# The feed-forward part of an attention block in another order: three chunks of gates at the head, other PSUM banks, and GpSimd on the even gates

## The reference

```python
x = x + layernorm(attention(layernorm(x), ...))
z = layernorm(x)
h = silu((z @ w1.T) * w1_s) * ((z @ w2.T) * w2_s)    # 128 -> 512, the gates
h = gelu((h @ h1.T) * h1_s)                          # 512 -> 512, layer 1
h = gelu((h @ h2.T) * h2_s)                          # 512 -> 512, layer 2
x = x + layernorm((h @ w3.T) * w3_s)                 # 512 -> 128, layer 3
```

## Time and profile before

| | us |
|---|---|
| median of 3 runs (lowest to highest) | 326.47 (325.59 to 327.27) |
| the profiled execution's own time | 327.04 |
| its span, first to last instruction | 325.2 |
| TensorE busy, share of the span | 283.9 (87%) |
| VectorE busy | 217.7 (67%) |
| ScalarE busy | 212.3 (65%) |
| GpSimd busy | 45.2 (14%) |

### The profile page before, as it was taken

The page is one execution under the profiler, slowest core; times in us unless marked ns, Lnnn a source line. Parts: engine busy times, 40 slices in busy tenths (PEclk is TensorE's granted clock), DMA queues, the critical chain, the costliest instruction groups (busy, mean ns, idle before and its releaser), DMA issues.

```text
span 325.2 us, 5036 instructions
## 1 busy us (share of the span) xinstructions
PE 283.9 (87%) x1844; PEld 186.9 (57%) x1844; DVE 217.7 (67%) x451; ACT 212.3 (65%) x313; POOL 45.2 (14%) x52
## 2 busy tenths in 40 slices
PE   8859699989999999999999966789997979699980
PEld 7644363646565555555555533346885758488870
DVE  3855355888789788897888956936558343554485
ACT  2431246678786787857878599547796576767750
POOL 3200400000001001010010137203202110300111
PEclk9985558999999999999999997559999798989997
DMA  6889800533031254522212000000000000010012
GB/s 160 260 248 245 283 2 24 183 109 100 27 89 54 67 194 171 174 87 67 78 31 62 1 3 0 1 0 2 1 2 0 0 0 0 2 32 0 1 35 69
DMA packets 22748, 23.29 MB, mean 72 GB/s; under 512 B 3745, under 2 KB 19905, under 8 KB 22465
## 3 DMA queue, kind: packets, MB, share of 16 engines
q1 hardware_dynamic: 21872, 22.38, 23.5%
q10 hardware_dynamic: 848, 0.54, 0.6%
HBM read 15.93 MB, written 6.68 MB: 70 GB/s over the span
## 4 chain that ended last, share of the span: by engine, by line
PE 52%; DVE 16%; ACT 11%; DMA 8%; issue 6%; SPq 4%; POOL 1%; ACTq 0%; POOLq 0%
PE place L1335 9%; PE place L1336 9%; PE place L1154 8%; PE pv L1204 7%; DVE mx L643 6%; ACT ring L916 5%; PE place L1144 4%; PE place L1180 3%; SPq L429 3%; DMA raw<-ext 2%; PE pv L1335 2%; DVE stats L569 2%; PE pv L1336 2%; DMA k_first<-z_parts 2%; DMA k_parts<-z_parts 2%
## 5 line engine op out<-in xcount | busy, mean ns | idle before, releaser
L643 DVE TENSOR_REDUCE mx<-place 128x4 f32<-128x1024 f32 x64 | 78.3, 1223 | 26.9 <-PE place L1154 25.7
L916 ACT ACTIVATE ring<-place 128x1024 f32<-128x1024 f32 x64 | 65.6, 1026 | 7.8 <-PE place L1191 5.7
L1154 PE MATMUL place<-room,identr 128*128 128x512 f32 x128 | 52.2, 492 | 3.6 <-ACT room L882 3.1
L923 ACT COPY place<-raw 128x1024 f32<-128x1024 f32 x40 | 40.8, 1021 | 16.0 <-DVE mx L643 16.0
L503 POOL TENSOR_TENSOR rstd<-mv,mhalf 128x2 f32<-128x2 f32 (+1 forms) x26 | 21.5, 827 | 205.4 <-DVE mv L577 205.4
L1335 PE MATMUL place<-room,w_hi 128*128 128x512 f32 (+1 forms) x108 | 42.6, 397 | 3.6 <-ACT ring L1026 2.9
L1336 PE MATMUL place<-room,w_hi 128*128 128x512 f32 (+1 forms) x108 | 41.9, 391 | 0.0
L1204 PE MATMUL pv<-ring,vx 128*9 128x256 f32 x512 | 37.0, 411 | 2.0 <-ACT ring L916 1.9
L1144 PE MATMUL place<-room 33*128 33x256 f32 x256 | 31.3, 325 | 8.4 <-ACT ring L916 4.0
L1180 PE MATMUL place<-room 33*128 33x256 f32 x256 | 34.2, 348 | 4.8 <-ACT place L923 3.3
L767 DVE TENSOR_TENSOR room<-ring,room 128x512 fp32r<-128x512 f32 x32 | 21.9, 691 | 22.7 <-ACT room L1028 22.7
(11 more groups left out here) (129 smaller groups left out, 395.7 us busy)
## 6 DMA issues: line engine op xcount, KB each, us to landing
raw<-ext SPq DMA_DIRECT2D x8, 384.0 KB, 7.3
room<-q_parts SPq DMA_DIRECT2D x48, 64.0 KB
room<-k_parts SPq DMA_DIRECT2D x48, 64.0 KB
w_lo<-h SPq DMA_DIRECT2D x2, 1024.0 KB, 5.0
q_parts<-w_hi SPq DMA_DIRECT2D x4, 256.0 KB, 3.1
k_parts<-w_hi SPq DMA_DIRECT2D x2, 512.0 KB, 3.4
xs<-x SPq DMA_DIRECT2D x3, 256.0 KB, 6.3
w_lo<-w SPq DMA_DIRECT2D x3, 256.0 KB, 2.8
```

Of the source, the lines that this page charges most:

```text
L643: nc.vector.tensor_reduce(mx[:, s // RPAIRS, :, :, s % RPAIRS].rearrange("p i k -> p k i"), max_tile(b * PAIRS + s)[:, :, :].rearrange("p ...
L916: nc.scalar.activation(probs[:, s % PRING, :, :, :].rearrange("p k j n -> p (k j n)"), score_tile(b * PAIRS + s)[:, :, :].rearrange("p k n ...
L923: nc.scalar.copy(score_tile(i)[:, :, :].rearrange("p k (j n) -> p k j n", j=2), pair_windows(raw[:, :, :], i % PAIRS)).then_inc(bias_set, 1)
L1154: last = mm(max_tile(b * PAIRS + s)[:, half, :], identr[:, :], windows(table_hi[:, 2 * s + half, :], 0, P, 2, S), start=False, stop=True, ...
```

## The change

The work is the same: as many matmuls, products, gelus and lo parts. What changes:

- TensorE takes the gates of chunks 0, 1 and 2 at the head, with layer 1 of chunk 0 among them one tile at a time. Layer 2 of chunk 1 and layer 1 of chunk 2 no longer have gates inside, but for layer 1 of chunk 2, which has gates 3.2 and 3.3 after its first tile. `norm_T` comes after the first tile of layer 2 of chunk 1.
- The tiles of the layers use other banks, in turn, and so wait for other readers; the slots and halves follow.
- For even gates GpSimd makes hi as well as lo (a copy with a cast, then the subtraction). ScalarE casts only the odd ones.
- VectorE's and ScalarE's lists follow TensorE's order. ScalarE switches tables between silu and gelu twice less, and two switches are asked for early by an activation of one column (`table_ahead`).

The core of the diff (the tuples, GpSimd's function, VectorE's list, ScalarE's list, what gates and layers wait for, TensorE's list):

```diff
-G_SLOT, A1_SLOT, A2_SLOT = (0, 1, 3, 0), (3, 2, 2, 1), (0, 1, 3, 2)
-G_HALF, A1_HALF, A2_HALF = (0, 1, 1, 1), (0, 1, 0, 1), (0, 0, 0, 1)
+G_SLOT, A1_SLOT, A2_SLOT = (0, 1, 2, 1), (3, 0, 0, 3), (1, 3, 2, 1)
+G_HALF, A1_HALF, A2_HALF = (0, 1, 0, 1), (1, 0, 0, 1), (1, 0, 0, 1)
...
-        A1_BANK = ((4, 5, 6, 0), (1, 2, 3, 4), (4, 5, 6, 4), (5, 6, 0, 1))
-        A2_BANK = ((5, 6, 4, 5), (6, 4, 5, 6), (2, 3, 4, 5), (6, 0, 1, 2))
-        Y3_BANK, BACK_BANK = (3, 4), (5, 6)
+        A1_BANK = ((4, 5, 6, 0), (1, 2, 3, 4), (6, 4, 5, 0), (1, 2, 3, 6))
+        A2_BANK = ((5, 6, 0, 1), (2, 3, 4, 5), (4, 5, 0, 1), (2, 3, 6, 4))
+        Y3_BANK, BACK_BANK = (5, 0), (1, 2)
...
-            def gate_low(c):
+            def gate_parts(c):
                 for k in range(0, NK, 2):
-                    pool.wait_ge(g_hi_act, c * NK + k + 1)
+                    pool.wait_ge(gate_set, c * NK + k + 1)
                     hi, lo = parts_of(G_SLOT[c], k)
+                    nc.gpsimd.tensor_copy(hi, act_f[:, G_HALF[c], k, :]).then_inc(g_hi_pool, 1)
+                    pool.wait_ge(g_hi_pool, c * (NK // 2) + k // 2 + 1)
                     nc.gpsimd.tensor_tensor(lo, act_f[:, G_HALF[c], k, :], hi.bitcast(F32),
                                             ALU.subtract).then_inc(g_lo_pool, 1)
...
-            gate_low(1)
+            gate_parts(0)
+            gate_parts(1)
+            gate_parts(2)
             inv_std((B - 1) * 2 + NU + 1, TPB)
             inv_std((B - 1) * 2 + NU + 2, TPB)
-            gate_low(2)
-            gate_low(3)
+            gate_parts(3)
...
+            def gate_product(c, k):
+                dve.wait_ge(silu_done, c * NK + (k + 1))
+                if c == 2:
+                    wait_gate_low(dve, 0, k)
+                elif c == 3:
+                    dve.wait_ge(a2_lo_set, k + 1)
+                nc.vector.scalar_tensor_tensor(
+                    out=act_f[:, G_HALF[c], k, :], in0=bank[GBANK[k % 2][1]], scalar=hs[:, 1, k:k + 1],
+                    in1=gate[:, k % 2, :], op0=ALU.mult, op1=ALU.mult).then_inc(gate_set, 1)
+            def gate_low(c, k):
+                dve.wait_ge(g_hi_act, c * (NK // 2) + k // 2 + 1)
+                hi, lo = parts_of(G_SLOT[c], k)
+                nc.vector.tensor_tensor(lo, act_f[:, G_HALF[c], k, :], hi.bitcast(F32),
+                                        ALU.subtract).then_inc(g_lo_dve, 1)
+            gate_product(0, 0)
+            gate_product(0, 1)
+            gate_product(0, 2)
+            gate_low(0, 1)
+            gate_product(0, 3)
+            gate_product(1, 0)
+            gate_low(0, 3)
+            gate_product(1, 1)
+            gate_product(1, 2)
+            gate_low(1, 1)
             weigh(B - 1, 0)
-            gates(1)
+            gate_product(1, 3)
+            gate_product(2, 0)
+            gate_low(1, 3)
+            gate_product(2, 1)
             weigh(B - 1, 1)
+            gate_product(2, 2)
+            gate_low(2, 1)
+            gate_product(2, 3)
+            gate_low(2, 3)
             layer_low(0, 0)
-            layer_low(1, 0)
             attn_moments(B - 1)
-            layer_low(0, 1, (0, 1))
+            layer_low(1, 0, (0, 1))
             residual(B - 1)
-            layer_low(0, 1, (2, 3))
+            layer_low(1, 0, (2, 3))
             second_norm(B - 1)
+            layer_low(0, 1)
+            layer_low(1, 1, (0, 1))
             z_low(B - 1)
-            gates(2)
-            layer_low(1, 1)
-            gates(3)
+            layer_low(1, 1, (2, 3))
+            gate_product(3, 0)
+            gate_product(3, 1)
+            gate_product(3, 2)
+            gate_low(3, 1)
+            gate_product(3, 3)
+            gate_low(3, 3)
...
-            gates(0)
-            gates(1)
-            layer(0, 0)
+            def table_ahead(function):
+                nc.scalar.activation(table_loaded[:, :], mhalf[:, 0:1], function)
+            for n in range(3 * NK):
+                gate_silu(n // NK, n % NK)
+                if n % 2 == 0 and n > 0:
+                    gate_high((n - 1) // NK, (n - 1) % NK)
+            gate_high(2, NK - 1)
+            layer(0, 0, (0, 1))
             keep_onT(B - 1)
+            layer(0, 0, (2, 3))
             layer(1, 0)
             layer(0, 1)
+            layer(1, 1, (0,))
             keep_zT(B - 1)
-            gates(2)
-            layer(1, 1)
+            layer(1, 1, (1, 2, 3))
+            table_ahead(ACT.Silu)
+            gate_silu(3, 0)
+            gate_silu(3, 1)
             keep_y3T(0)
-            gates(3)
+            gate_silu(3, 2)
+            gate_high(3, 1)
+            gate_silu(3, 3)
+            gate_high(3, 3)
+            table_ahead(ACT.Gelu)
             keep_y3(0, first=True)
             layer(2, 0)
             keep_y3T(1)
...
-                if c == 2 and k < 2:
-                    pe.wait_ge(a1_set, (5, 7)[k])
+                if c == 3 and k < 2:
+                    pe.wait_ge(a2_set, (4, 6)[k])
...
+                free = (((None, 0), (None, 0), (None, 0), (gate_set, 11)),
+                        ((gate_set, 11), (gate_set, 12), (gate_set, 12), (a1_set, 1)),
+                        ((a2_set, 2), (a2_set, 7), (a2_set, 8), (gate_set, 15)),
+                        ((gate_set, 15), (gate_set, 16), (gate_set, 16), (a1_set, 9)))[c][k]
...
+                free = (((a1_set, 2), (a1_set, 3), (a1_set, 4), (a1_set, 5)),
+                        ((a1_set, 6), (a1_set, 7), (a1_set, 8), (a2_set, 1)),
+                        ((a1_set, 10), (a1_set, 11), (a1_set, 12), (a1_set, 13)),
...
                 whole(gate, 0, exact)
+                whole(gate, 1, exact, (0, 1))
                 pe.wait_ge(z_lo_set, B - 1)
                 back(B - 1, 0)
-                whole(gate, 1, exact, (0, 1))
-                with_gates(layer1, 0, 1, exact)
+                gate(1, 2, exact)
+                layer1(0, 0, exact)
+                gate(1, 3, exact)
+                gate(2, 0, exact)
+                layer1(0, 1, exact)
+                back(B - 1, 1)
+                whole(gate, 2, exact, (1, 2))
+                layer1(0, 2, exact)
+                gate(2, 3, exact)
                 heads_T(B - 1)
-                whole(layer1, 1, exact)
+                layer1(0, 3, exact)
+                whole(layer1, 1, exact, (0, 1))
                 project(B - 1)
+                whole(layer1, 1, exact, (2, 3))
                 whole(layer2, 0, exact)
+                layer2(1, 0, exact)
                 pe.wait_ge(y_read, B)
                 norm_T(B - 1)
-                whole(gate, 2, exact, (0, 1))
-                with_gates(layer2, 1, 2, exact)
+                whole(layer2, 1, exact, (1, 2, 3))
                 pe.wait_ge(z_hi_set, B)
                 pe.wait_ge(z_lo_set, B)
                 layer3(0, exact, first=True)
                 whole(gate, 3, exact, (0, 1))
+                layer1(2, 0, exact)
                 tokens_back(0)
-                with_gates(layer1, 2, 3, exact)
+                whole(gate, 3, exact, (2, 3))
+                whole(layer1, 2, exact, (1, 2, 3))
                 layer3(1, exact)
```

More of the change, by code:

```diff
@@ L267, in build @@
         g_hi_act = sem("g_hi_act")
+        g_hi_pool = sem("g_hi_pool")
         g_lo_pool = sem("g_lo_pool")
@@ L1425, in last_tokens_back @@
                 last.then_inc(last_back[half], 1)
-            def with_gates(layer, c, g, exact):
-                for k in range(NK):
-                    layer(c, k, exact)
-                    if k < 2:
-                        gate(g, 2 + k, exact)
-                        if g == 1 and k == 1:
-                            back(B - 1, 1)
             def whole(layer, c, exact, outputs=range(NK)):
```

62 lines of the change are left out of this document (13 added, 49 removed).

## The result

The changed kernel takes 313.31 us (median of 4 runs, 312.59 to 316.57) where the kernel before takes 326.63 (4 runs, 325.59 to 327.27): a ratio of 0.9615, 95% interval 0.9542 to 0.9687. On another chip it was 314.52 (6 runs, 313.14 to 317.11) to 326.08: 0.965 (0.9611 to 0.969). All ratios here leave out executions over 1.5% above the fastest of their kernel. The forecast was 314.5. The profiled execution took 312.59 us, its span is 310.7, and its mean granted clock 0.925 instead of 0.900.

The account below looks back on a forecast made before the run. TensorE's holes and the half clock behind them were taken as the bound: 13.65 us removed, 0.45 and 0.95 added, so 12.25 less, giving 314.5 us. The range was 313.0 to 317.6.

Parts of the forecast that it names:

- What bounds it: TensorE, feed-forward part: three holes of 8.54 us in all, half clock behind them 4.86, restarts 0.25; 13.65 us removed.
- the 4.86 for half clock: TensorE behind the three holes: eight or nine matmuls at half clock each, costing 1.57, 1.59 and 1.70 us.
- project's wait: TensorE at project: a new wait of 0.85 us for ScalarE's copy onT, plus 0.1 for the restart.
- The gates don't hold TensorE: TensorE's head up to project: products arrive before gates need them; no hole, 0.3 to 1.2 us to spare.
- back costs 0.45: TensorE near gate 1.1: the back's four transposes no longer lie in a hole and add 0.45 us.
- What is late next: After project: norm_T, banks and ScalarE's copies; none late, three places with 0.3 to 1.0 us of slack.
- GpSimd's casts: New 128x512 casts on GpSimd at the head: 0.6 us each, 1.9 per even gate with the subtraction.
- The drain at a table switch: ScalarE's table switches: the skill counts about 1.38 us of drain beside 1.28 of load; the forecast saw no drain.
- the clock did not fall at project: First rival, TensorE at project: the clock falls after the wait, price 1.6 us, 316.1; chance 0.11.
- The gelu was not late: Second rival, ScalarE: first gelu later than 3.45 us after silu 2.3; if 1.7 later, 317.8; chance 0.06.
- GpSimd is busy for 6.33 of 16.00 us: Third rival: GpSimd becomes the bound of the head, 327 us or more; chance 0.03.
- No hole moved: Fourth rival: another bank or copy is late by as much, with no gain beyond 1.6 us; chance 0.04.

Follow-up runs that it names:

- bank_alone: Kernel before, with only the fourth tile of layer 1 of chunk 2 moved to a bank that a silu frees: 0.9861 of the kernel before.
- onT_after4: Changed kernel with ScalarE's copy for project behind four gelus instead of two: project waits 3.17 us; 2.71 us more than with the copy behind three.
- before_busy: Kernel before, with two transposes of the last attention batch but one issued eleven times to fill a TensorE wait: 0.9981 of the kernel before.
- onT_early: Changed kernel with ScalarE's copy for project ahead of the table load and first gelu: 312.34 us, 0.9597 of the kernel before.
- back_and_onT_early: onT_early with the first back again ahead of gate 1.1, as in the kernel before: 88.55 us from gate 1.1 to the end.
- bank_undone: Changed kernel with the fourth tile of layer 1 of chunk 2 again in a gelu's bank: 314.21 us; 1.80 longer from gate 1.1 to the end.
- act_high: Changed kernel with ScalarE casting all gates' high parts and GpSimd none: 90.20 us from gate 1.1 to the end, 0.66 longer.
- after_again: Changed kernel unaltered, run again on another chip: 314.52 us; 89.53 from gate 1.1 to the end.
- no_table_ahead: Changed kernel without its two early table requests: 89.70 us from gate 1.1 to the end, within 0.2 of the changed kernel.
- onT_after3: Changed kernel with ScalarE's copy for project behind three gelus instead of two: 316.15 us; project waits 1.93.
- after: The changed kernel's first run and its profile: median 313.31 us, profiled execution 312.59.
- onT_early_busy: onT_early with two transposes of the last attention batch but one issued eleven times to fill a TensorE wait: 313.03 us.
- onT_early_2: onT_early repeated unaltered, as baseline for onT_early_busy: 311.48 us.

## Why the prediction was right

By its own steps, from gate 1.1 on, where the two profiles can be compared:

- **What bounds it** (holes on TensorE and half clock behind them): right. All three holes went, as did all three phases of half clock. The list up to the last-but-one tokens_back came 12.16 sooner (76.59 us after gate 1.1 before, 64.43 now), for 12.25 forecast. bank_alone took one of the holes away alone and got 3.90. onT_after4 made one and paid for both parts of it. For the other two holes the cause is read from the rows, and no run tests it by itself. The second part is a little less sure than the sum had it, since before_busy's first hole went without: the 4.86 for half clock is what the profiled execution paid, and another may pay 1.6 less.
- **project's wait**: 0.95 forecast, 0.96 measured, and 0.97 came back when onT_early took it away.
- **The gates don't hold TensorE**: right from gate 1.1 on. But for project, no step between products is over 0.34 us there (for 0.23), and those above 0.3 stand at gate 1.1's start and behind transposes.
- **back costs 0.45**: nearly. The first took 0.58 (222.19 to 222.66, and 0.11 more for the matmul behind it), the second 0.44. Before it lay in a hole; back_and_onT_early put it there again and gained nothing.
- **What is late next**: nothing, as said. norm_T stands at 32.85 us behind gate 1.1 (forecast 32.65). bank_undone and act_high show how thin this is: a bank or a cast placed otherwise brings 1.8 and 0.3 us back. The one size that was off, without effect, is batch 7's chain: 6.5 us for 7.6.
- **GpSimd's casts**: 0.6 us was right for one by itself, and 1.00 is true beside a VectorE lo part:

```profile
217.15 0.61 POOL L545 CAST room<-ring 128x512 fp32r<-128x512 f32 x1 [7.45 <-DVE ring L782]
...
219.91 1.00 POOL L545 CAST room<-ring 128x512 fp32r<-128x512 f32 x1 [0.77 <-DVE ring L782]
```

```profile
219.76 0.68 DVE L789 TENSOR_TENSOR room<-ring,room 128x512 fp32r<-128x512 f32 x1
```

  The lo part began first and kept its 0.68; the cast, which began at 219.91, met it for 0.53 and took 0.39 longer. The forecast had only looked at VectorE losing. The cast lost in six of the eight cases, each with a lo part begun 0.15 ahead, so that an even gate took GpSimd 2.4 us and not the 1.9 of the forecast; none of it is seen on TensorE. By the Trainium skill's rule (SBUF — State Buffer, Who interferes with whom) the second waits for the first. The trace agrees on which one loses; the 0.39 is less than the 0.53 of overlap.
- **The drain at a table switch**: by the Trainium skill (ScalarE: Activation LUTs, What ACT_TABLE_LOAD costs) about 1.38 us would have stood beside each load. The rows have 235.88 + 0.62 = 236.50 to the load's 236.52, and its end at 237.80 to the gelu's 237.81: none, at this switch as before the change.
- **The rivals**: the clock did not fall at project; in the one profile each of the longer waits there it stays at 1.93 and falls at 3.17. The gelu was not late. GpSimd is busy for 6.33 of 16.00 us from 226 to 242. No hole moved.

What the prediction did not have is the chance ahead of gate 1.1. It had gate 1.1 at 223.55 us, as before. In the twelve profiles without repeated transposes it starts anywhere from 220.1 to 224.2. The first median, 313.31, is 1.2 under the forecast, and the second, 314.52, on it. I do not count the first as a better gain, and that the second falls on the forecast is in part luck. The change is the yardstick's 12.11 against the profiled execution of before, and 10.7 against one in which half clock is missing behind one hole.

## What to carry to other kernels

Price a hole in a full matmul stream with what stands behind it: here waits of 2.40 to 3.17 us cost some 1.6 us of half clock more in eight cases of nine, while waits of up to 1.93 cost only themselves in the profiles taken. When operations with two tables are interleaved, place the copies that another engine waits for ahead of the table load, and give a tile that comes early a bank whose reader comes early; each was a few lines here, worth 1.0 to 1.3 and 1.8 to 3.9 us. Where one execution differs from the next by more than the edit, measure a stretch within the profile that begins behind the place where they part.

## What the runs showed of the hardware

- **Which waits half clock followed.** In the full stream of the feed-forward part the clock was at 1.00 behind waits of 0.51, 0.70, 1.50 and 1.93 us, at half behind 2.40, 2.76, 2.89 and 3.17, but behind one of 2.76 (before_busy) it stayed at 1.00 (as the timeline gives them). These are cases and no limit.
- **Ahead of that part it falls and returns otherwise in each execution.** It was back near 210, or between 216 and 219; in after_again and before_busy it came back near 204, fell again, and was back at 221 and 223; in no_table_ahead and onT_after3 it had fallen by 194, behind waits of 1.38 and 1.39, the second of which left it at 1.00 in after. A late return costs 1.9 to 2.4 us up to gate 1.1 (128.5 or 130.4 to 130.9 us from the row near 93 us), of it 1.1 to 1.5 between gates 0.0 and 1.1, which take 6.9 us at full clock. This is not all that spreads one kernel's times: 3.2 us more arise in the first 93 us.
- **A TensorE kept at full clock where ScalarE sets the pace waits longer at the next place**: in onT_early_busy's profile 2.28 us for 0.63 in onT_early_2's, and half clock followed.
- **GpSimd's cast of 128x512** takes 0.61 us, and up to 1.01 when a VectorE operation with two SBUF inputs began 0.15 us ahead of it.
